# An attention and gated feed-forward stack in fp32 on one core: a norm's clamp and square moved to ScalarE, two tiled matmul stages made neighbours, and two copies reordered

## Chip, cores, metric

One Trainium2 chip, one of its cores. The time is the device time of one launch in microseconds (us), median over runs. Everything is computed in fp32.

## The reference

`x` is (4, 512, 128): four sequences (B) of 512 tokens. A small cross attention with a context comes first (the prologue here, under 3% of the time). Then a stack of six layers runs, each with a windowed attention of 16 heads of 64 and a gated feed-forward:

```python
def l2norm(t):
    return t / jnp.maximum(jnp.linalg.norm(t, axis=-1, keepdims=True), 1e-12)

def attn_layer(x, Wqkv, qs, ksc, Wo):
    q, k, v = jnp.split(x @ Wqkv, 3, -1)          # split in 16 heads of 64
    q = l2norm(q) * qs
    k = l2norm(k) * ksc
    q = q * cos * scale + rotate_half(q) * sin * scale
    k = k * cos * inv + rotate_half(k) * sin * inv
    out = local_attention(q, k, v)                # windows of 32, look back one window, softmax
    return out @ Wo

def ffn_layer(x, g, bln, W1, b1, W2, b2):
    a, gate = jnp.split((layernorm(x) * g + bln) @ W1 + b1, 2, -1)
    return a * gelu(gate) @ W2 + b2

for i in range(6):
    x = attn_layer(shift_tokens(x), ...) + x
    x = ffn_layer(shift_tokens(x), ...) + x
```

## The kernel before

The stack is cut into 192 units: 24 groups (a layer and a sequence), each of 8 units (4 tiles of 128 tokens times 2 halves of 8 heads). It is a software pipeline written out by hand: slot `n` of a long loop issues stages of several units. TensorE computes q and k of unit n, v of unit n, applies the attention weights of unit n-5 (`attend`), transposes o of n-6, makes the scores of n-3, transposes p of n-4, and then transposes k and q of n-2. `s = n % 8` is the slot within a group. Some slots have one more piece of TensorE work of the layer around the attention: s=0 `mean`, s=1 `variance`, s=2 and s=6 `project_out`, s=3 three `up` matmuls for the gate and one for a, s=4 and s=5 one `up` each, s=7 `down` (and every fourth group `fold_bias` in s=2). A 128x512 matmul in fp32 shows as two records in the profile.

`scores` and `attend` are the tiled stages: 16 matmuls each, whose weights are 32 columns wide and go to one of four column positions of the array (`tile_position=(0, WIN * w)`), shown as 128*32 in the profile. All other matmuls and transposes use the whole array, 128*128.

Other engines, in each slot:
- ScalarE (ACT): `copy_qT`, `norm_seed` (an inverse square root as Ln and Exp), `copy_v`, `copy_oT`, `squares` (the squares of q and k from PSUM), `copy_pT`, `copy_kB`, `fill_mask`, `exponentials`; in s=1 `square_d`, in s=2 `rstd_seed` (three operations), in s=3 three Gelus and two table loads.
- VectorE (DVE): `sum_p`, `newton` (a Newton step on the seed), `scale_k`, `scale_q`, `maxima`, `invert_sum`, `less_maxima`, `sum_squares`, `clamp_squares`, `scale_o` and the layer's sums and norms.
- GpSimd (POOL): the rotation of k and q, six operations a unit.
- SyncE (SP): the DMAs that spread v over the windows (`vs` to `vw`), 8 or 10 a unit, and the weights.

PSUM has two pairs of banks for q and k (`qk_bank0`, `qk_bank1`), one for scores (`sc_bank`) and a ring of three (`ring_bank`) that all other results share in the order of TensorE's program: the n-th use takes bank n % 3 and waits until the use three before it has been copied out (`ring_read`). So the order of TensorE's stages also says whose copy each of them waits for. `queries_keys(n)` waits until `scale_q(n-2)` has read its bank. Engines work through their programs in order, each at its own pace, held together by semaphores.

## Time and profile before

| | us |
|---|---|
| median of 3 runs (1822.89 to 1824.75) | 1823.85 |
| the profiled execution, its own time | 1824.23 |
| its span in the profile | 1822.2 |

| engine | busy us | share of the span |
|---|---|---|
| PE (TensorE matmul) | 1750.3 | 96% |
| DVE (VectorE) | 1619.0 | 89% |
| POOL (GpSimd) | 1500.4 | 82% |
| ACT (ScalarE) | 1327.5 | 73% |

The span divides in a prologue of some 50 us, the 192 slots that start a unit, and a tail in which the last units leave the pipeline. A matmul's end in the profile is modelled, so consecutive ones overlap; the distance from one start to the next is what it costs. PEld is the loading of weights, beside PE.

### The profile page before, as it was taken

Reading aid. Unit: us, or ns where it says so; the run is one execution under the profiler, and the core shown is the slowest. Engines: PE = TensorE matmul, PEld = TensorE weight load, DVE = VectorE, ACT = ScalarE, POOL = GpSimd, SP = SyncE. Lnnn points to the kernel's source line nnn. Section 1 sums busy time; section 2 is a strip of 40 time slices with the busy share of each in tenths; the row PEclk is TensorE's granted clock in tenths of the full one; section 3 lists DMA queues with packets and bytes.
Section 4 is the critical chain, followed back from the end, with each engine's and each line's share of the span. In section 5 each row is a group of like instructions: output and inputs, shape, how many; then the busy total and the mean of one; then the engine's idle time right before and its main releaser. Section 6 shows DMA issues by size and latency. Waiting matters only on the chain.

```text
span 1822.2 us, 48666 instructions
## 1 busy us (share of the span) xinstructions
PE 1750.3 (96%) x18122; PEld 1116.2 (61%) x18122; DVE 1619.0 (89%) x2782; ACT 1327.5 (73%) x2362; POOL 1500.4 (82%) x1204
## 2 busy tenths in 40 slices
PE   7699999999999999999999999999999999999986
PEld 6356666666666666666666666666666666666663
DVE  7799998999999989989999999899999998988874
ACT  3577877877778778778777777787776877877763
POOL 4799888888888888988888888888888888888860
PEclk9999999999999999999999999999999999999998
DMA  4132222222222222322223222222222222222221
GB/s 114 28 87 67 68 71 57 60 73 76 71 63 69 63 66 71 76 65 68 63 56 81 72 70 72 54 63 73 75 72 62 68 58 58 59 71 56 56 64 29
DMA packets 155273, 120.59 MB, mean 66 GB/s; under 512 B 42607, under 2 KB 151457, under 8 KB 154913
## 3 DMA queue, kind: packets, MB, share of 16 engines
q1 hardware_dynamic: 155041, 117.48, 25.1%
q8 instruction: 147, 2.41, 0.6%
q14 instruction: 85, 0.70, 0.1%
HBM read 18.79 MB, written 1.05 MB: 11 GB/s over the span
## 4 chain that ended last, share of the span: by engine, by line
PE 77%; DVE 13%; POOL 5%; issue 3%; SPq 1%; ACT 1%; DMA 1%; DVEq 0%; POOLq 0%; ACTq 0%
PE qk_bank L376 17%; PE ring_bank L448 10%; PE ring_bank L472 9%; PE ring_bank L389 8%; PE sc_bank L423 7%; PE ring_bank L516 6%; PE ring_bank L436 4%; PE ring_bank L399 3%; PE ring_bank L527 3%; PE ring_bank L461 3%; PE ring_bank L410 3%; DVE rn L842 2%; DVE step L837 2%; DVE o L898 2%; DVE qkn L858 2%
## 5 line engine op out<-in xcount | busy, mean ns | idle before, releaser
L1053 POOL TENSOR_TENSOR turned<-qkn,tables 128x512 f32<-128x512 f32 x384 | 489.3, 1274 | 209.8 <-DVE qkn L850 201.5
L1060 POOL TENSOR_TENSOR turned<-qkn,tables 128x512 f32<-128x512 f32 x384 | 496.7, 1294 | 0.0
L376 PE MATMUL qk_bank<-wqkv,xT 128*128 128x512 f32 x768 | 366.5, 600 | 18.8 <-DVE qkn L858 18.6
L1089 POOL TENSOR_TENSOR turned<-turned 128x512 f32<-128x512 f32 x192 | 255.0, 1328 | 15.1
L1096 POOL TENSOR_TENSOR turned<-turned 128x512 f32<-128x512 f32 x192 | 245.1, 1277 | 15.1
L448 PEld LDWEIGHTS ring_bank<-vw,pT 128*32 128x32 f32 x6144 | 156.6, 110 | 143.8 <-issue 143.7
L654 ACT ACTIVATE kB<-ring_bank 64x512 f32<-64x512 f32 x384 | 225.3, 587 | 23.5 <-PE ring_bank L410 21.2
L824 DVE TENSOR_REDUCE ss<-sq 128x16 f32<-128x1024 f32 x192 | 232.0, 1208 | 6.8 <-ACT sq L618 6.8
L627 ACT ACTIVATE vs<-ring_bank 128x512 f32<-128x512 f32 x192 | 114.7, 598 | 163.1 <-PE ring_bank L389 153.4
L898 DVE TENSOR_TENSOR o<-ring_bank,rr 128x512 f32<-128x512 f32 x192 | 132.1, 688 | 104.2 <-PE ring_bank L448 101.3
L389 PE MATMUL ring_bank<-wqkv,xT 128*128 128x512 f32 x384 | 216.1, 645 | 1.6 <-DVE x L978 1.6
L664 ACT ACTIVATE sc_bank<-mask_f 128x512 f32<-128x512 f32 x192 | 114.5, 596 | 136.0 <-DVE pr L873 135.6
L448 PE MATMUL ring_bank<-vw,pT 128*32 128x128 f32 x6144 | 208.4, 276 | 0.1
L423 PE MATMUL sc_bank<-kB,qT 128*32 128x128 f32 x6144 | 207.5, 276 | 0.3
L376 PEld LDWEIGHTS qk_bank<-wqkv,xT 128*128 128x128 f32 x768 | 131.2, 191 | 121.7 <-issue 93.4
L618 ACT ACTIVATE sq<-qk_bank 128x1024 f32<-128x1024 f32 x192 | 198.0, 1031 | 0.0
L423 PEld LDWEIGHTS sc_bank<-kB,qT 128*32 128x32 f32 x6144 | 156.0, 109 | 34.7 <-issue 34.7
L472 PE MATMUL ring_bank<-oT,wo 128*128 128x256 f32 x768 | 173.8, 379 | 0.0
L461 PEld LDWEIGHTS ring_bank<-ident,o 128*128 128x128 f32 x768 | 95.5, 141 | 102.1 <-issue 83.9
L472 PEld LDWEIGHTS ring_bank<-oT,wo 128*128 128x128 f32 x768 | 142.2, 190 | 18.1 <-DVE uT L956 0.8
L516 PE MATMUL ring_bank<-xnT,w 128*128 128x512 f32 x288 | 143.3, 609 | 8.5 <-DVE xnT L947 7.3
L850 DVE TENSOR_TENSOR qkn<-qk_bank,rn 128x512 f32<-128x512 f32 x192 | 132.9, 692 | 20.7 <-DVE rn L842 0.9
(169 smaller groups left out, 3129.3 us busy)
## 6 DMA issues: line engine op xcount, KB each, us to landing
vw<-vs SPq DMA_DIRECT2D x1152, 64.0 KB, 2.1
vw<-vs SPq DMA_DIRECT2D x672, 32.0 KB, 1.9
wqkv<-in_L_ffn_Wqkv_dram SPq DMA_DIRECT2D x20, 384.0 KB, 3.5
wo<-in_L_ffn_Wo_dram SPq DMA_DIRECT2D x20, 128.0 KB, 3.3
w<-in_L_ffn_W_dram SPq DMA_DIRECT2D x6, 341.0 KB, 3.4
wqkv<-in_L_ffn_Wqkv_dram SPq DMA_DIRECT2D x1, 1536.0 KB, 9.5
x<-in_x_dram SPq DMA_DIRECT2D x2, 512.0 KB, 4.7
out_dram<-x SPq DMA_DIRECT2D x4, 256.0 KB, 2.3
```

The costliest lines, as they stand in the source:

```text
L376: mm = pe.matmul(QK[u % 2][:, i * UW:(i + 1) * UW], tok, wqkv[:, layer % 2, cut:cut + UW], start=True, stop=True)
L389: pe.matmul(RING[i % RINGS][:, :], xT[:, b, t * P:(t + 1) * P], wqkv[:, layer % 2, cut:cut + UW], start=True, stop=True).then_inc(ring_mad ...
L423: mm = pe.matmul(heads(SC_BANK[WIN * w:WIN * (w + 1), k * P:(k + 1) * P]), qT[:, u % 2, k, WIN * w:WIN * (w + 1)], kB[:, HP * half + k, :, ...
L448: mm = pe.matmul(heads(RING[i % RINGS][WIN * w:WIN * (w + 1), k * P:(k + 1) * P]), pT[:, u % 2, k, WIN * w:WIN * (w + 1)], vw[:, u % 2, w, ...
L472: mm = pe.matmul(RING[i % RINGS][:, 0:HALF], wo[:, layer % 2, k, :], oT[:, k, HALF * h:HALF * (h + 1)], start=(k == 0), stop=(k == KO - 1))
L516: pe.matmul(RING[i % RINGS][:, :], w1[:, DFF * j + k * P:DFF * j + (k + 1) * P], xnT[:, :], start=True, stop=True).then_inc(ring_made[i % ...
L654: ev = act.activation(kB[64 * h:64 * h + 64, HP * half:HP * half + HP, h, WIN + P * t:WIN + P * t + P], RING[i % RINGS][64 * h:64 * h + 64 ...
L824: dve.tensor_reduce(ss[:, :], heads(sq[:, :]), AX.X, ALU.add).then_inc(ss_done, 1)
L1053: return pool.tensor_tensor(heads(turned[:, u % 2, 2 * i, :]), heads(qkn[:, u % 2, i * UW:(i + 1) * UW]), table.unsqueeze(1).to_broadcast( ...
L1060: return pool.tensor_tensor(halves(turned[:, u % 2, 2 * i + 1, :]), halves(qkn[:, u % 2, i * UW:(i + 1) * UW])[:, :, ::-1, :], table.rearr ...
L1089: pool.tensor_tensor(q, q, turned[:, u % 2, 1, :], ALU.add).then_inc(q_summed, 1)
L1096: pool.tensor_tensor(k, k, turned[:, u % 2, 3, :], ALU.add).then_inc(k_summed, 1)
```

## The change

Four edits:
- The norm's seed. `clamp_squares` (VectorE's maximum with the smallest norm) goes. ScalarE now reads the sums `ss` itself: Relu(ss - min), Ln with the minimum added back through its bias, Exp, and then the half square of the seed, `half_sq`. VectorE's Newton step has two operations in place of three. Each unit so has four small ScalarE operations in place of two, and two small VectorE operations in place of four. `ss` has two buffers.
- TensorE's order in a slot: v now comes ahead of `attend`, and `scores` right behind it, ahead of the transposes of o.
- ScalarE's order: the copy of p right behind that of o, and `squares` behind the copy of k.
- `vs` has seven slots in place of six, so `copy_v` waits for a DMA of one unit earlier. VectorE's `sum_p` of the next unit stands ahead of `scale_o`, except in s=3.

```diff
-VS = 6
+VS = 7
@@ tensor
                 queries_keys(n)
+                values(n)
                 attend(n - 5)
-                values(n)
+                scores(n - 3)
                 transpose_o(n - 6)
-                scores(n - 3)
                 transpose_p(n - 4)
@@ scalar
-                act.wait_ge(ssm_done, u + 1)
-                act.activation(lnn[:, u % 2, :], ssm[:, u % 2, :], ACT.Ln, scale=LN_SHIFT).then_inc(ln_done, 1)
-                act.wait_ge(ln_done, u + 1)
-                act.activation(seed[:, u % 2, :], lnn[:, u % 2, :], ACT.Exp, bias=shift_back[:, 0:1],
-                               scale=-0.5).then_inc(seed_done, 1)
+                act.wait_ge(ss_done, u + 1)
+                act.activation(above, ss[:, u % 2, :], ACT.Relu, bias=floor[:, 0:1]).then_inc(seed_part, 1)
+                act.wait_ge(seed_part, 4 * u + 1)
+                act.activation(above, above, ACT.Ln, bias=floor[:, 1:2], scale=LN_SHIFT).then_inc(seed_part, 1)
+                act.wait_ge(seed_part, 4 * u + 2)
+                act.activation(sd, above, ACT.Exp, bias=shift_back[:, 0:1], scale=-0.5).then_inc(seed_part, 1)
+                act.wait_ge(seed_part, 4 * u + 3)
+                act.activation(half_sq[:, u % 2, :], sd, ACT.Square, scale=0.5 ** 0.5).then_inc(seed_part, 1)
...
                 copy_oT(n - 6)
-                squares(n)
                 copy_pT(n - 4)
...
                 copy_kB(n - 2)
+                squares(n)
@@ vector
-                dve.scalar_tensor_tensor(out=step[:, :], in0=sd, scalar=-0.5, in1=sd,
-                                         op0=ALU.mult, op1=ALU.mult).then_inc(newton_done, 1)
-                dve.wait_ge(newton_done, 2 * u + 1)
-                dve.tensor_tensor(step[:, :], step[:, :], ssm[:, u % 2, :], ALU.mult).then_inc(newton_done, 1)
-                dve.wait_ge(newton_done, 2 * u + 2)
-                dve.scalar_tensor_tensor(out=r, in0=step[:, :], scalar=1.5, in1=sd,
-                                         op0=ALU.add, op1=ALU.mult).then_inc(rn_done, 1)
+                dve.wait_ge(seed_part, 4 * u + 4)
+                dve.scalar_tensor_tensor(out=step[:, :], in0=ss[:, u % 2, :], scalar=NORM_MIN ** 2, in1=half_sq[:, u % 2, :],
+                                         op0=ALU.max, op1=ALU.mult).then_inc(newton_done, 1)
+                dve.wait_ge(newton_done, u + 1)
+                dve.scalar_tensor_tensor(out=rn[:, u % 2, :], in0=step[:, :], scalar=1.5, in1=seed[:, u % 2, :],
+                                         op0=ALU.subtract, op1=ALU.mult).then_inc(rn_done, 1)
...
-                clamp_squares(n - 1)
...
+                if s != 3:
+                    sum_p(n - 4)
                 scale_o(n - 5)
```

TensorE's program, the start of a slot in the middle of the stack, before (qk_bank: q and k; `wqkv,xT` into a ring bank: v; `vw,pT`: attend; `ident,o`, `ident,pr`, `ident,turned`: transposes of o, p, and k; sc_bank: scores):

```order
L376 MATMUL qk_bank1<-wqkv,xT 128x512 x2
L448 MATMUL ring_bank0<-vw,pT 32x128 x16
L389 MATMUL ring_bank1<-wqkv,xT 128x512
L461 MATMUL ring_bank2<-ident,o 128x128 x4
L423 MATMUL sc_bank<-kB,qT 32x128 x16
L436 MATMUL ring_bank0<-ident,pr 128x128 x4
L410 MATMUL ring_bank1<-ident,turned 128x128 x4
```

The same place in the changed kernel:

```order
L374 MATMUL qk_bank1<-wqkv,xT 128x512 x2
L387 MATMUL ring_bank0<-wqkv,xT 128x512
L446 MATMUL ring_bank1<-vw,pT 32x128 x16
L421 MATMUL sc_bank<-kB,qT 32x128 x16
L459 MATMUL ring_bank2<-ident,o 128x128 x4
L434 MATMUL ring_bank0<-ident,pr 128x128 x4
L408 MATMUL ring_bank1<-ident,turned 128x128 x4
```

The two tiled stages now touch. In the ring, p's transposes took the bank of `attend` (read by VectorE's `scale_o`) and now take the bank of v (read by ScalarE's `copy_v`); k's transposes took v's bank and now take that of `attend`.

ScalarE's program from the copy of k in slot s=0 to that of v in s=1, before:

```order
L654 ACTIVATE kB<-ring_bank0 64x4x128 x2
L664 ACTIVATE sc_bank<-mask_f 128x512
L671 ACTIVATE pr<-pr 128x512
L645 ACTIVATE qT<-ring_bank1 128x512
L634 ACTIVATE lnn<-ssm 128x16
L636 ACTIVATE seed<-lnn,shift_back 128x16
L698 ACTIVATE dsq<-dT 128x512
L627 ACTIVATE vs<-ring_bank0 128x512
```

The same stretch in the changed kernel, without the copy of k at its head:

```order
L616 ACTIVATE sq<-qk_bank0 128x1024
L666 ACTIVATE sc_bank<-mask_f 128x512
L673 ACTIVATE pr<-pr 128x512
L647 ACTIVATE qT<-ring_bank1 128x512
L633 ACTIVATE lnn<-ss,floor 128x16
L635 ACTIVATE lnn<-lnn,floor 128x16
L637 ACTIVATE seed<-lnn,shift_back 128x16
L639 ACTIVATE half_sq<-seed 128x16
L700 ACTIVATE dsq<-dT 128x512
L625 ACTIVATE vs<-ring_bank2 128x512
```

The squares of q and k and two more small operations stand in this stretch now, between the copy of k and that of v.

VectorE's program from the sum of squares in s=1 to the scaling of k, before:

```order
L824 TENSOR_REDUCE ss<-sq 128x16
L830 TENSOR_TENSOR ssm<-ss,norm_min 128x16
L898 TENSOR_TENSOR o<-ring_bank2,rr 128x512
L880 TENSOR_REDUCE rs<-pr 128x8
L837 SCALAR_TENSOR_TENSOR step<-seed 128x16
L840 TENSOR_TENSOR step<-step,ssm 128x16
L842 SCALAR_TENSOR_TENSOR rn<-step,seed 128x16
L850 TENSOR_TENSOR qkn<-qk_bank0,rn 128x512
```

And changed:

```order
L827 TENSOR_REDUCE ss<-sq 128x16
L874 TENSOR_REDUCE rs<-pr 128x8
L892 TENSOR_TENSOR o<-ring_bank0,rr 128x512
L833 SCALAR_TENSOR_TENSOR step<-ss,half_sq 128x16
L836 SCALAR_TENSOR_TENSOR rn<-step,seed 128x16
L844 TENSOR_TENSOR qkn<-qk_bank0,rn 128x512
```

The sum over p (`rs`) comes ahead of the scaling of o, which waits for `attend`, and two small operations are gone.

## Rows read from the trace of the kernel before

**Rows 1.** Windows, 400 to 1600 us: busy time of PE, PEld, DVE, ACT, POOL; clock; DMA.
```profile
400.00:1600.00 1200.00, 1184.54 (x12409) 752.65 (x12408) 1100.57 (x1842) 911.85 (x1625) 1027.81 (x818) 1.00 0.26 67
```

**Rows 2.** The page: the span.
```profile
span 1822.2 us, 48666 instructions
```

**Rows 3.** Groups by line and shape, 400 to 1600 us: busy, mean ns, idle before.
```profile
L376 PE MATMUL qk_bank<-wqkv,xT 128*128 128x512 f32 x535 | 254.8, 599 | 12.5 <-DVE qkn L858 12.5
L830 DVE TENSOR_TENSOR ssm<-ss,norm_min 128x16 f32<-128x16 f32 x134 | 68.4, 510 | 4.6
```

**Rows 4.** Timeline of PE, one slot (s=4): start, us, engine, line, operation, tiles, count.
```profile
926.74 1.88 PE L376 MATMUL qk_bank<-wqkv,xT 128*128 128x512 f32 x4
928.55 1.08 PE L448 MATMUL ring_bank<-vw,pT 128*32 128x128 f32 x32
929.57 1.12 PE L389 MATMUL ring_bank<-wqkv,xT 128*128 128x512 f32 x2
930.53 0.60 PE L461 MATMUL ring_bank<-ident,o 128*128 128x128 f32 x4
931.06 1.08 PE L423 MATMUL sc_bank<-kB,qT 128*32 128x128 f32 x32
932.07 0.66 PE L436 MATMUL ring_bank<-ident,pr 128*128 128x128 f32 x4
932.56 0.60 PE L410 MATMUL ring_bank<-ident,turned 128*128 128x128 f32 x4
...
934.29 0.59 PE L376 MATMUL qk_bank<-wqkv,xT 128*128 128x512 f32 x1
```

**Rows 5.** Timeline of PE, s=3: matmuls and transposes without a tiled neighbour.
```profile
924.59 1.88 PE L516 MATMUL ring_bank<-xnT,w 128*128 128x512 f32 x4
926.30 0.60 PE L399 MATMUL ring_bank<-ident,turned 128*128 128x128 f32 x4
```

**Rows 6.** Timeline of PE, narrow windows: first and last four records of one attend.
```profile
936.11 0.32 PE L448 MATMUL ring_bank<-vw,pT 128*32 128x128 f32 x4
...
936.90 0.29 PE L448 MATMUL ring_bank<-vw,pT 128*32 128x128 f32 x4
937.12 0.70 PE L389 MATMUL ring_bank<-wqkv,xT 128*128 128x512 f32 x1
```

**Rows 7.** Timelines of DVE and of POOL, the same moment in s=5.
```profile
940.11 1.14 DVE L842 SCALAR_TENSOR_TENSOR rn<-step,seed 128x16 f32<-128x16 f32 x1
939.91 1.30 POOL L1089 TENSOR_TENSOR turned<-turned 128x512 f32<-128x512 f32 x1
```

**Rows 8.** Waits, 400 to 1600 us: in total, times, longest.
```profile
ACT vs L627 <- PE ring_bank L389: 102.7, 118, 2.7
DVE o L898 <- PE ring_bank L448: 66.1, 70, 2.2
```

**Rows 9.** Timeline of ACT, from s=0 into s=1.
```profile
969.54 1.19 ACT L654 ACTIVATE kB<-ring_bank 64x512 f32<-64x512 f32 x2 [0.64 <-PE ring_bank L410]
...
971.90 0.60 ACT L645 ACTIVATE qT<-ring_bank 128x512 f32<-128x512 f32 x1
972.59 0.22 ACT L634 ACTIVATE lnn<-ssm 128x16 f32<-128x16 f32 x1
972.84 0.31 ACT L636 ACTIVATE seed<-lnn,shift_back 128x16 f32<-128x16 f32 x1
973.05 0.61 ACT L698 ACTIVATE dsq<-dT 128x512 f32<-128x512 f32 x1
974.21 0.60 ACT L627 ACTIVATE vs<-ring_bank 128x512 f32<-128x512 f32 x1 [0.54 <-DMA vw<-vs]
```

**Rows 10.** Timeline of ACT, from s=3 into s=4.
```profile
921.30 1.03 ACT L618 ACTIVATE sq<-qk_bank 128x1024 f32<-128x1024 f32 x1
...
929.23 0.58 ACT L645 ACTIVATE qT<-ring_bank 128x512 f32<-128x512 f32 x1
930.79 0.60 ACT L627 ACTIVATE vs<-ring_bank 128x512 f32<-128x512 f32 x1 [0.53 <-PE ring_bank L389]
```

More of the change, by code:

```diff
@@ L107, in build @@
         turned = sb("turned", [P, 2, 4, UW])
-        ss = sb("ss", [P, 2 * HU])
-        ssm = sb("ssm", [P, 2, 2 * HU])
-        lnn = sb("lnn", [P, 2, 2 * HU])
+        ss = sb("ss", [P, 2, 2 * HU])
+        lnn = sb("lnn", [P, 2 * HU])
         seed = sb("seed", [P, 2, 2 * HU])
+        half_sq = sb("half_sq", [P, 2, 2 * HU])
         step = sb("step", [P, 2 * HU])
@@ L114, in build @@
         shift_back = sb("shift_back", [P, 1])
-        norm_min = sb("norm_min", [P, 2 * HU])
+        floor = sb("floor", [P, 2])
         qT = sb("qT", [P, 2, HP, P])
@@ L221, in build @@
         ss_done = sem("ss_done")
-        ssm_done = sem("ssm_done")
-        ln_done = sem("ln_done")
-        seed_done = sem("seed_done")
+        seed_part = sem("seed_part")
         newton_done = sem("newton_done")
@@ L624, in copy_v @@
                 if u >= VS - 2:
-                    act.wait_ge(vw_dma[u % 2], vw_count(u - VS + 2))
+                    act.wait_ge(vw_dma[(u - VS + 2) % 2], vw_count(u - VS + 2))
                 act.wait_ge(ring_made[i % RINGS], i // RINGS + 1)
@@ L632, in norm_seed @@
                     return
-                act.wait_ge(ssm_done, u + 1)
-                act.activation(lnn[:, u % 2, :], ssm[:, u % 2, :], ACT.Ln, scale=LN_SHIFT).then_inc(ln_done, 1)
-                act.wait_ge(ln_done, u + 1)
-                act.activation(seed[:, u % 2, :], lnn[:, u % 2, :], ACT.Exp, bias=shift_back[:, 0:1],
-                               scale=-0.5).then_inc(seed_done, 1)
+                above, sd = lnn[:, :], seed[:, u % 2, :]
+                act.wait_ge(ss_done, u + 1)
[6 more added lines that the diff above has]
+                act.activation(half_sq[:, u % 2, :], sd, ACT.Square, scale=0.5 ** 0.5).then_inc(seed_part, 1)
             def copy_qT(u):
@@ L756, in _ @@
             dve.memset(shift_back[:, :], 0.5 * float(np.log(LN_SHIFT))).then_inc(cst_ready, 1)
-            dve.memset(norm_min[:, :], NORM_MIN ** 2)
+            dve.memset(floor[:, 0:1], -NORM_MIN ** 2)
+            dve.memset(floor[:, 1:2], LN_SHIFT * NORM_MIN ** 2)
             dve.memset(mean_w[:, :], 1.0 / C).then_inc(cst_ready, 1)
@@ L823, in sum_squares @@
                 dve.wait_ge(sq_done, u + 1)
-                dve.tensor_reduce(ss[:, :], heads(sq[:, :]), AX.X, ALU.add).then_inc(ss_done, 1)
-            def clamp_squares(u):
-                if not 0 <= u < UNITS:
-                    return
-                dve.wait_ge(ss_done, u + 1)
-                dve.tensor_tensor(ssm[:, u % 2, :], ss[:, :], norm_min[:, :], ALU.max).then_inc(ssm_done, 1)
+                dve.tensor_reduce(ss[:, u % 2, :], heads(sq[:, :]), AX.X, ALU.add).then_inc(ss_done, 1)
             def newton(u):
@@ L982, in _ @@
                 g, s = n // UPG, n % UPG
-                sum_p(n - 5)
                 newton(n - 2)
@@ L990, in _ @@
                 if s == 1:
+                    finish(g - 3)
                     centre(g - 2)
@@ L1013, in _ @@
                     layer_norm(g - 2)
-                if s == 1:
-                    finish(g - 3)
+                    sum_p(n - 4)
         @block.gpsimd
```

2 lines of the change are left out of this document (removed).

## Prediction, on record before the run

> **What bounds the kernel now.** I read the windows first. Between 400 and 1600 us TensorE is busy 1184.5 of 1200 us at the full clock (1.00, so 2.4 GHz), VectorE 1100.6, GpSimd 1027.8, ScalarE 911.9 [rows 1]. The windows' sum says that TensorE is the bound and that only its own work, or its stalls, are worth time. The profiled execution took 1824.2 us, 2.0 more than its span [rows 2] and 0.4 more than the median; I work from 1824.2.
>
> Next the pace. q and k take four records a slot, and 535 of them lie in 1200 us [rows 3], so a slot takes 1200 / 133.75 = 8.97 us on average, 71.8 us a group of 8. Little of that is waiting: 1200 - 1184.5 = 15.5 us idle, of which 12.5 lie ahead of q and k and are put down to VectorE's scaling of q (L858) [rows 3]. A record runs some 0.16 us past the point where the next could start (0.60 us long, 0.44 apart in the transposes [rows 4, 5]), so some 28 such waits hide about 4.5 us more. Together 20 us in 16.7 groups, 1.2 a group; I use 1.3.
>
> Then TensorE's timeline of one slot, where the reader is to look at distances between starts, not at lengths. Four passes of 512 columns take 926.30 - 924.59 = 1.71 us where no tiled stage is near, and four transposes 926.74 - 926.30 = 0.44 [rows 4, 5]. Next to the tiled stages they take more:
> - q and k ahead of `attend`: 928.55 - 926.74 = 1.81, 0.10 more [rows 4].
> - v behind it: 930.53 - 929.57 = 0.96 for two passes, against 0.86: 0.10 more.
> - o's transposes ahead of `scores`: 931.06 - 930.53 = 0.53, 0.09 more. p's behind: 932.56 - 932.07 = 0.49, 0.05 more.
> - Inside `attend`, the first and last quadruples of records start 0.79 us apart, seven steps of 0.113; but from the last to v it is 937.12 - 936.90 = 0.22, 0.11 more [rows 6].
>
> So each trip into tiling and back costs about 0.10 in, 0.11 out and another 0.05 to 0.10 on the first full stage. A slot makes two trips.
>
> **The change, step by step.**
>
> *Tiled stages side by side.* One exit (0.11), the surcharge on v behind it (0.10) and one entry (0.09) go, and about 0.03 of the slower first quadruple: 0.33 us a slot, 192 x 0.33 = **63 us**. The exit behind `scores` and the entry behind v stay. From below: if only the visible surcharges on v and o vanish, 0.19 x 192 = 36 us. From above 0.11 + 0.10 + 0.10 + 0.10 = 0.41, 79 us. I take 0.33, since each term has its row. The Trainium skill, in "TensorEngine Tiling (Array Packing)", section "Key Properties", says that changing the tiling mode drains TensorE while moving among tiles of one mode does not. By that rule the two stages, both 128x32, need no drain between them, and the trace agrees with it in the surcharges.
>
> *VectorE.* The clamp of 0.51 us on average goes [rows 3], and one of three Newton steps. These are tiny operations that are long when they meet GpSimd: the last Newton step started at 940.11, ran 1.14 and ended at 941.25 beside a GpSimd operation that ended at 941.21 [rows 7]. So a chain of two costs 0.4 to 1.35 us, where one of three could meet GpSimd twice. Also `sum_p` (0.6 us) now fills the time that `scale_o` waited for `attend`, 66.1 us in 1200 [rows 8]. On the other side `attend` ends 0.87 us later in the slot (it starts at 1.72 + 0.96 = 2.68 instead of 1.81). In a short slot (s=0, 1, 4, 5; 934.29 - 926.74 = 7.55 us before, 7.22 after) the round from q and k over `attend`, o, Newton, and scaling k and q is then 3.9 + 0.6 + 1.3 + 1.4 = 7.2 us: as long as TensorE's slot. VectorE's stalls mostly vanish: **31 us** (24 x 1.3) come back, and I charge 0.15 a group again below.
>
> *ScalarE.* It gets two more small operations, and their dependence is a chain. Ln takes 0.22, Exp 0.31 [rows 9]; with starts 0.25 apart before, four of them with bias take 1.1 to 1.3, I take 1.2 against 0.55. The Trainium skill has a rule against this step: "ScalarE: Activation LUTs", section "Rules for kernel authors", gives relu and max to VectorE and budgets about 0.3 us for an ACTIVATE with a pointer as bias, which would make four of them about 1.2 us as well, an estimate by that page; the rows bear the price out, but VectorE's clamp was 0.51 here, not cheaper.
>
> ScalarE as a whole has room: 911.9 of 1200 busy, 102.7 of it idle ahead of the copy of v [rows 1, 8]. What counts is when the copy of v is done. Before, v's bank was next used by k's transposes; now p's transposes take it, which stand earlier. And the squares, 1.03 us [rows 10], now lie between the copies of k and v. I walk the places, with times from the slot's start; TensorE after the change: v 1.72, `attend` 2.68, `scores` 3.58, o's transposes 4.57, p's 5.06, k's 5.50.
>
> - s=1. In s=0 `mean` (0.86) stands ahead of k's transposes, so these start at 6.36, run 0.60 [rows 4], and ScalarE copies k from 7.0. From there to the copy of qT it was 971.90 - 969.54 = 2.36 us [rows 9]; now the squares add 0.93. Then qT 0.6, four small operations 1.2, `square_d` 0.6, copy of v 0.6: 7.0 + 2.36 + 0.93 + 3.0 = 13.3, less 7.22 is 6.1. p's transposes want the bank at 5.06: **1.0 us** of stall.
> - s=4. Before, qT's copy started 929.23 - 926.74 = 2.49 into the slot, right after the table load [rows 4, 10]. The squares now lie ahead of it, and it starts at 3.45 and ends at 4.05; `scores` want it at 3.58: 0.5. Then 3.95 + 1.2 + 0.6 = 5.8 for the copy of v against 5.06 + 0.5: 0.25. Together **0.75**. Before there was room: `scores` started at 4.32, v's copy at 930.79 still waited 0.53 for TensorE [rows 4, 10].
> - s=3. `rstd_seed` in s=2 stands behind the squares; v's copy ends about 5.2: **0.15**.
> - s=5, 0.15 from VectorE as above. s=2, 6, 7 are long (9 to 10 us) and cover everything.
>
> That is 2.05 a group, times 24: **49 us**. From below nothing, if ScalarE keeps ahead; from above, with 1.3 us for the four and 0.1 more on every copy, 3 us a group, 72 us.
>
> *Seven slots for v.* ScalarE waited 0.54 us for the DMA at 974.21 [rows 9]. In a shorter slot this wait would grow; with a unit more of distance it goes. Cover for anything left is TensorE's wait above. I cost it at nothing. If the DMA were late all the same, the copy of v and p's transposes are late next.
>
> Sum: 1824.2 - 63 - 31 + 49 = 1779.
>
> **Rivals.**
> - *ScalarE keeps up.* Its stalls at s=1 and s=4 don't come, as short slots give back what long ones hold. For it: 288 us idle in 1200. Against: the walk, slot by slot. 1824 - 63 - 31 = 1730, or 1761 if VectorE's stalls stay as they are. 0.2.
> - *ScalarE worse than walked*, stalls also in s=0 and s=5, as each short slot asks 6.5 to 6.8 us of it in 7.22: 3 us a group, 1802. 0.14.
> - *The drains don't go* (the surcharge belongs to new operands and not to the mode, so a smaller part goes): 0.1 a slot, 19 us, gives 1824 - 19 - 31 + 49 = 1823. For it: only one order of stages has ever been seen. Against: matmuls and transposes alternate elsewhere without any surcharge [rows 5]. 0.05.
> - *Slower: ScalarE becomes the bound of the short slots.* At the copy of v behind the chain of four. If each of the four took 0.5 us, its round of a short slot is 7.4 us and no slot is made up; at s=0, 1, 4 and 5 it costs about 1.1 each, 4.5 a group, 108 us: 1824 - 94 + 108 = 1838. It decides from (63 + 31) / 24 = 3.9 us of new stalls a group; Exp's 0.31 [rows 9] speaks against. 0.05. By the skill's rule that relu belongs on VectorE, this is the case that would follow.
>
> **How the numbers follow.** The forecast, 1765 to 1794, has 0.56. The range 1740 to 1805 takes in much of the first two rivals: about 0.8. A measurement of this kernel tells about 0.2% from no change. Faster by more than that: 0.56 + 0.2 + 0.14 and a little of the third, 0.92; within 0.2%: 0.03; slower: 0.05.
>
> **What would show it.** In TensorE's timeline: `attend` to `scores` about 0.90 us apart, `scores` to o's transposes 1.01, these then 0.49, v 0.96 ahead of `attend`; a slot without waits 0.33 shorter. In the waits: p's transposes on ScalarE's copy of v in s=1 and s=4, `scores` on qT in s=4. In the groups: four small operations of ScalarE at 0.2 to 0.3. Wrong would be: a first quadruple of `scores` as slow as before, no waits of TensorE on the copy of v, or waits on VectorE's scaling of q as often as before.

## The result, and the profile after

The changed kernel takes 1780.22 us (median of 4 runs, 1776.14 to 1781.41) against 1824.3 (now 4 runs, 1822.89 to 1830.04): ratio 0.9744, 95% interval 0.9726 to 0.9761. The forecast was 1779. The profiled execution took 1781.41 us.

The page of the changed kernel: span and busy time of each engine.

```profile
span 1779.4 us, 48666 instructions
...
PE 1709.0 (96%) x18122; PEld 1136.8 (64%) x18122; DVE 1370.6 (77%) x2399; ACT 1396.2 (78%) x2746; POOL 1499.9 (84%) x1204
```

VectorE falls from 89% to 77%, ScalarE rises from 73% to 78%: the two have passed each other. The window from 400 to 1600 us, to be read against [rows 1]:

```profile
400.00:1600.00 1200.00, 1187.20 (x12855) 788.41 (x12853) 949.06 (x1624) 987.60 (x1950) 1060.25 (x843) 1.00 0.26 69
```

TensorE is as busy as before, yet it issues more: 12855 records for 12409. What the change took out was busy time (drains inside matmuls) as well as idle time, so the busy share can't show the gain; the pace can. Groups of the same stretch, which answer to [rows 3]:

```profile
L374 PE MATMUL qk_bank<-wqkv,xT 128*128 128x512 f32 x552 | 259.9, 593 | 0.0
L833 DVE SCALAR_TENSOR_TENSOR step<-ss,half_sq 128x16 f32<-128x16 f32 x137 | 46.8, 342 | 6.5 <-ACT half_sq L639 5.3
L836 DVE SCALAR_TENSOR_TENSOR rn<-step,seed 128x16 f32<-128x16 f32 x137 | 26.1, 191 | 4.7
...
L639 ACT ACTIVATE half_sq<-seed 128x16 f32<-128x16 f32 x138 | 29.8, 216 | 4.4
```

There are 552 records of q and k for 535, and nothing idle ahead of them: TensorE no longer waits for VectorE's scaling of q. Newton costs VectorE 0.53 us a unit (0.34 and 0.19). Of ScalarE's four small operations the half square takes 0.22 us and the other three 0.30 to 0.31. The waits, 400 to 1560 us, show where TensorE waits instead:

```profile
PE sc_bank L421 <- ACT qT L647: 6.3, 17, 0.4
PE ring_bank L434 <- ACT vs L625: 5.9, 16, 0.4
```

Each comes once a group, at s=1 (vs) or s=4 (qT). TensorE's timeline of a slot without a wait (s=5), against [rows 4]:

```profile
916.34 1.88 PE L374 MATMUL qk_bank<-wqkv,xT 128*128 128x512 f32 x4
918.05 1.02 PE L387 MATMUL ring_bank<-wqkv,xT 128*128 128x512 f32 x2
919.01 1.08 PE L446 MATMUL ring_bank<-vw,pT 128*32 128x128 f32 x32
919.90 1.06 PE L421 MATMUL sc_bank<-kB,qT 128*32 128x128 f32 x32
920.89 0.66 PE L459 MATMUL ring_bank<-ident,o 128*128 128x128 f32 x4
921.38 0.60 PE L434 MATMUL ring_bank<-ident,pr 128*128 128x128 f32 x4
921.82 0.60 PE L408 MATMUL ring_bank<-ident,turned 128*128 128x128 f32 x4
```

Read the distances from start to start: q and k to v 1.71 (`attend` behind q and k took 1.81), v to `attend` 0.96, `attend` to `scores` 0.89 (1.02 to whatever followed it before), `scores` to o's transposes 0.99, these 0.49, p's 0.44 (0.49 before). And s=1, whose q and k start at 880.69, with its wait:

```profile
885.38 0.66 PE L459 MATMUL ring_bank<-ident,o 128*128 128x128 f32 x4
886.40 0.66 PE L434 MATMUL ring_bank<-ident,pr 128*128 128x128 f32 x4 [0.36 <-ACT vs L625]
```

p's transposes follow those of o by 1.02 instead of 0.49. The record of idle time says 0.36; the other 0.17 is the part by which o's record (0.66 long) runs past the point where the next stage could start. That is why I count stalls by starts. Two smaller ones stand beside it: in this slot `scores` start 1.01 behind `attend` instead of 0.89, as the copy of qT (ScalarE, below) ends only at 884.22, and k's transposes 0.49 behind p's instead of 0.44. The other end of this wait stands in ScalarE's timeline, from s=0 into s=1, against [rows 9]:

```profile
880.46 1.19 ACT L656 ACTIVATE kB<-ring_bank 64x512 f32<-64x512 f32 x2 [0.59 <-PE ring_bank L408]
881.67 1.02 ACT L616 ACTIVATE sq<-qk_bank 128x1024 f32<-128x1024 f32 x1
...
883.63 0.59 ACT L647 ACTIVATE qT<-ring_bank 128x512 f32<-128x512 f32 x1
884.11 0.30 ACT L633 ACTIVATE lnn<-ss,floor 128x16 f32<-128x16 f32 x1
...
885.25 0.61 ACT L700 ACTIVATE dsq<-dT 128x512 f32<-128x512 f32 x1
885.77 0.58 ACT L625 ACTIVATE vs<-ring_bank 128x512 f32<-128x512 f32 x1
```

From k's copy on nothing is idle, and the copy of v ends at 886.35, 0.05 us before p's transposes start.

For all that follows I took from each trace the start of q and k in every slot; the table gives mean slot lengths in the steady part of the stack, in us (one profiled execution of each kernel).

| kernel | s=0 | 1 | 2 | 3 | 4 | 5 | 6 | 7 | group |
|---|---|---|---|---|---|---|---|---|---|
| before | 7.56 | 8.04 | 10.55 | 10.41 | 7.55 | 8.21 | 10.25 | 9.27 | 71.84 |
| changed | 7.22 | 7.92 | 10.24 | 9.84 | 7.95 | 7.36 | 9.96 | 9.10 | 69.59 |
| no_join | 7.51 | 7.93 | 10.43 | 10.15 | 7.87 | 7.51 | 10.10 | 9.23 | 70.73 |
| order_back | 7.55 | 7.61 | 10.47 | 10.14 | 7.86 | 7.55 | 10.15 | 9.28 | 70.62 |
| order_only | 7.86 | 8.34 | 10.40 | 11.28 | 7.86 | 8.16 | 10.06 | 9.29 | 73.26 |
| seed_back | 7.45 | 8.69 | 10.34 | 11.36 | 8.10 | 7.88 | 10.07 | 9.30 | 73.20 |
| three_newton | 7.51 | 8.68 | 10.34 | 10.51 | 7.95 | 8.16 | 10.06 | 9.10 | 72.31 |
| squares_early | 7.87 | 7.86 | 10.30 | 10.27 | 7.87 | 7.86 | 9.95 | 9.10 | 71.08 |
| vs6 | 7.22 | 8.20 | 10.54 | 10.00 | 7.94 | 7.36 | 10.26 | 9.10 | 70.61 |
| o_first | 7.22 | 7.93 | 10.24 | 10.16 | 7.95 | 7.88 | 10.06 | 9.10 | 70.53 |
| late_dsq | 7.22 | 7.63 | 10.25 | 9.98 | 7.96 | 7.36 | 9.96 | 9.10 | 69.45 |
| dsq_dve | 7.22 | 7.57 | 10.24 | 10.45 | 7.95 | 7.36 | 9.96 | 9.11 | 69.86 |
| v_dve | 7.22 | 7.50 | 10.24 | 10.41 | 7.94 | 7.36 | 9.95 | 9.10 | 69.72 |
| v_dve_qT | 7.22 | 7.53 | 10.24 | 10.49 | 7.36 | 7.53 | 9.95 | 9.10 | 69.42 |

### The profile page after: what moved, and what is told of

It is laid out like the page before. It is cut to its first block, busy times and chain, and to the rows that moved or that the text cites. A ratio compares the mean times of both kernels' runs of the same rounds, so it can differ in the third digit from the quotient of the medians.

```text
span 1779.4 us, 48666 instructions
## 1 busy us (share of the span) xinstructions
PE 1709.0 (96%) x18122; PEld 1136.8 (64%) x18122; DVE 1370.6 (77%) x2399; ACT 1396.2 (78%) x2746; POOL 1499.9 (84%) x1204
## 4 chain that ended last, share of the span: by engine, by line
PE 75%; ACT 13%; POOL 5%; issue 4%; DVE 3%; ACTq 0%; DVEq 0%; POOLq 0%
PE qk_bank L374 13%; PE ring_bank L470 9%; PE sc_bank L421 8%; PE ring_bank L446 8%; PE ring_bank L387 7%; PE ring_bank L514 5%; PE ring_bank L459 5%; PE ring_bank L434 5%; PE ring_bank L408 4%; PE ring_bank L525 4%; PE ring_bank L397 3%; ACT sq L616 2%; ACT L718 2%; POOL turned L1047 2%; POOL turned L1054 2%
## 5 line engine op out<-in xcount | busy, mean ns | idle before, releaser
L692 ACT ACTIVATE oT<-ring_bank 128x512 f32<-128x512 f32 x192 | 114.5, 596 | 179.5 <-PE ring_bank L459 179.3
L387 PE MATMUL ring_bank<-wqkv,xT 128*128 128x512 f32 x384 | 197.6, 596 | 0.0
L421 PEld LDWEIGHTS sc_bank<-kB,qT 128*32 128x32 f32 x6144 | 169.4, 110 | 19.6 <-issue 19.5
L470 PE MATMUL ring_bank<-oT,wo 128*128 128x256 f32 x768 | 177.8, 385 | 0.0
L874 DVE TENSOR_REDUCE rs<-pr 128x8 f32<-128x512 f32 x192 | 130.6, 680 | 28.0 <-ACT pr L673 25.8
L397 PEld LDWEIGHTS ring_bank<-ident,turned 128*128 128x128 f32 x768 | 92.9, 141 | 87.7 <-issue 47.3
```

The lines of the kernel that those rows point to most:

```text
L387: pe.matmul(RING[i % RINGS][:, :], xT[:, b, t * P:(t + 1) * P], wqkv[:, layer % 2, cut:cut + UW], start=True, stop=True).then_inc(ring_mad ...
L421: mm = pe.matmul(heads(SC_BANK[WIN * w:WIN * (w + 1), k * P:(k + 1) * P]), qT[:, u % 2, k, WIN * w:WIN * (w + 1)], kB[:, HP * half + k, :, ...
L470: mm = pe.matmul(RING[i % RINGS][:, 0:HALF], wo[:, layer % 2, k, :], oT[:, k, HALF * h:HALF * (h + 1)], start=(k == 0), stop=(k == KO - 1))
```

## Experiments

Diffs are against the changed kernel, but for order_only. "Ratio" is that to the kernel before in the same round of measurements (its medians there: 1827.02, 1829.27 and 1828.51 us), with its 95% interval. The changed kernel was measured in the first round only, and the kernel before moved by up to 5 us from round to round, so differences in us to the changed kernel of some 5 us or less say nothing.

### One piece undone at a time

**no_join**: `scores` back behind the transposes of o, so that the two tiled stages are apart again.

```diff
                 attend(n - 5)
-                scores(n - 3)
                 transpose_o(n - 6)
+                scores(n - 3)
```

> The changed kernel with one thing undone: the transposes of o stand between attend and scores again, v stays ahead of attend, and the banks of the ring stay as they are. Theory (the price belongs to each trip into and out of the tiled mode): a second trip comes back, an exit of 0.11 and 0.05 on the transposes of o, and an entry of 0.09 with 0.02 on the first quadruple, 0.27 us a slot and 52 us over 192 slots. Since scores start 0.6 us later, the wait for the copy of qT in s=4 (0.55 us a group, 13 us) goes in return. So 1780 + 52 - 13 = 1819, between 1812 and 1832. Rival (the surcharge came from v and o meeting new operands, not from the mode): at most 19 us more, under 1800. In the timeline of TensorE the theory wants 0.53 us for the transposes of o and about 0.16 more than 0.90 from attend to the next stage.

Measured: 1802.65 us, ratio 0.987 (0.9844 to 0.9896). TensorE's timeline of its slot s=0:

```profile
888.86 1.08 PE L446 MATMUL ring_bank<-vw,pT 128*32 128x128 f32 x32
889.88 0.66 PE L459 MATMUL ring_bank<-ident,o 128*128 128x128 f32 x4
890.46 1.08 PE L421 MATMUL sc_bank<-kB,qT 128*32 128x128 f32 x32
891.47 0.66 PE L434 MATMUL ring_bank<-ident,pr 128*128 128x128 f32 x4
```

`attend` takes 1.02 again, o's transposes 0.58 and `scores` 1.01. A slot without waits is 7.51 for 7.22, 0.29 where 0.27 was expected, so the trip has the price that was read. But it is worth 22 us in the whole (27 by the slots, 1.14 a group), between the expectation and its rival: in s=1 the slot is 7.92 with the join and 7.93 without, because ScalarE's copy of v sets its end either way, and s=4 even favours no_join by 0.08. Where TensorE waits for another engine, shorter work on TensorE is a longer wait.

**squares_early**: the squares back between the copies of oT and pT.

```diff
                 copy_oT(n - 6)
+                squares(n)
                 copy_pT(n - 4)
...
                 copy_kB(n - 2)
-                squares(n)
```

> The changed kernel with ScalarE's squares between the copies of o and of p, as before. Theory (each copy out of the ring gates a stage of TensorE): the stretch from k's copy to v's is 0.93 us shorter, so the stalls in s=1 and s=4 (1.5 us a group) go; but p's copy then ends 7.4 us into the slot, and in s=0, 1, 4 and 5 the transposes of q, which take p's bank, want it at 6.8: 0.65 us each, 2.6 a group. Net 1.1 us a group slower, 27 us: 1807, between 1795 and 1815. Rival (only v's copy matters): 36 us faster, 1745.

Measured: 1811.68 us, ratio 0.9914 (0.9884 to 0.9944), as expected. Its one large wait:

```profile
PE ring_bank L397 <- ACT pT L682: 21.6, 68, 0.7
```

68 times in 1200 us, four a group: in each short slot the transposes of q want the bank of p's transposes, whose copy now comes a unit of squares later. All four short slots are 7.86 to 7.87, so the stalls in s=1 and s=4 have not come on top: the new wait has taken their place.

**vs6**: six slots for v.

```diff
-VS = 7
+VS = 6
```

> The changed kernel with six slots for v, so that v's copy again waits for a DMA one unit younger. I costed the seventh slot at nothing before. Theory: with six the DMA lands 9.1 us after attend of the slot before ends (in the trace of the kernel before: 974.21 against an attend that ended near 965.1); attend now ends at 3.8, so v's copy can't start before 12.9 - 7.2 = 5.6 us behind a short slot. Then p's transposes wait 1.2 us, in s=1 and s=5, less what is there already: 1.2 to 1.8 us a group, 1808 to 1825. Rival (the cost is hidden behind the waits that are there): 1780 within 4.

Measured: 1801.52 us, ratio 0.985 (0.9821 to 0.9878); 21 us for an edit that touches one number, somewhat less than expected. Waits, of ScalarE and then of TensorE behind it:

```profile
ACT vs L625 <- DMA vw<-vs: 35.5, 42, 1.9
```
```profile
PE ring_bank L434 <- ACT vs L625: 18.2, 32, 1.3
```

With six slots the copy of v waits for the DMA of the unit four before it, with seven for that of five before, which is issued earlier. p's transposes wait for the copy twice as often as in the changed kernel. s=1, 2, 3 and 6 are longer by 0.28, 0.30, 0.16 and 0.30; the expectation had named s=1 and s=5, and s=5 is unchanged.

**seed_back**: the clamp on VectorE, the three Newton operations and two small ScalarE operations, as before, with the new orders.

```diff
-                act.activation(above, ss[:, u % 2, :], ACT.Relu, bias=floor[:, 0:1]).then_inc(seed_part, 1)
...
-                act.activation(half_sq[:, u % 2, :], sd, ACT.Square, scale=0.5 ** 0.5).then_inc(seed_part, 1)
+                act.activation(lnn[:, u % 2, :], ssm[:, u % 2, :], ACT.Ln, scale=LN_SHIFT).then_inc(ln_done, 1)
...
+                dve.tensor_tensor(ssm[:, u % 2, :], ss[:, :], norm_min[:, :], ALU.max).then_inc(ssm_done, 1)
```

> The changed kernel with the norm's seed as before: the clamp on VectorE, two small operations on ScalarE, three Newton operations on VectorE. All orders and the seven slots of v stay. Theory A (both engines matter): ScalarE's chain is 0.65 us shorter, so the stalls in s=1 and s=4 shrink from 0.72 and 0.77 us to about 0.1 and 0.3; but VectorE's round in a short slot becomes 3.9 + 0.6 + 2.0 + 1.4 = 7.9 us against TensorE's 7.22, and waits on the scaling of q of up to 0.7 us come back in some of the four short slots. Net between -0.3 and +1.3 us a group: 1775 to 1810, centre 1793. Theory B (ScalarE alone sets the stalls, VectorE has room): 24 us less, 1756. Theory C (the seed's move is what made the kernel faster): back to 1815 or more.

Measured: 1867.85 us, ratio 1.023 (1.0199 to 1.0261). The largest miss of the study, in the range of theory C and not of theory A: the seed is worth 88 us here, and without it the change would be a loss. VectorE's timeline in a short slot whose q and k start at 889.03 us:

```profile
892.95 0.69 DVE L898 TENSOR_TENSOR o<-ring_bank,rr 128x512 f32<-128x512 f32 x1 [0.70 <-PE ring_bank L448]
893.55 0.54 DVE L837 SCALAR_TENSOR_TENSOR step<-seed 128x16 f32<-128x16 f32 x1
...
894.33 1.13 DVE L842 SCALAR_TENSOR_TENSOR rn<-step,seed 128x16 f32<-128x16 f32 x1
...
896.18 0.68 DVE L858 TENSOR_TENSOR qkn<-qk_bank,rn 128x512 f32<-128x512 f32 x1
```

GpSimd's timeline of the same moment:

```profile
892.77 1.29 POOL L1061 TENSOR_TENSOR turned<-qkn,tables 128x512 f32<-128x512 f32 x1
894.14 1.29 POOL L1090 TENSOR_TENSOR turned<-turned 128x512 f32<-128x512 f32 x1
```

The first Newton operation ends at 894.09, with the first GpSimd operation (894.06); the third at 895.46, with the second (895.43). VectorE's scaling of q ends at 896.86. TensorE could go on at 896.4, 0.44 behind q's transposes (895.95), but its timeline reads:

```profile
896.92 1.98 PE L376 MATMUL qk_bank<-wqkv,xT 128*128 128x512 f32 x4 [0.37 <-DVE qkn L858]
```

The round that begins with `attend` is longer than TensorE's slot. The Trainium skill, "SBUF — State Buffer", section "SBUF: two separate sides", describes VectorE and GpSimd as holding a shared pair of ports exclusively for a whole instruction, a VectorE operation with two SBUF inputs among those concerned. In both cases above VectorE's operation ends 0.03 us behind GpSimd's, which agrees with it.

**three_newton**: only the half square goes back, as a third operation of VectorE's chain; ScalarE keeps three small operations and VectorE has no clamp.

```diff
-                act.activation(half_sq[:, u % 2, :], sd, ACT.Square, scale=0.5 ** 0.5).then_inc(seed_part, 1)
...
+                dve.scalar_tensor_tensor(out=half_sq[:, u % 2, :], in0=seed[:, u % 2, :], scalar=0.5, in1=seed[:, u % 2, :],
+                                         op0=ALU.mult, op1=ALU.mult).then_inc(newton_done, 1)
```

> The changed kernel with the half square of the seed back on VectorE: three small operations on ScalarE, three Newton operations on VectorE, the clamp stays gone. It splits the 88 us that putting back the whole seed cost (1780 to 1868). Theory (each small VectorE operation may run up to 1.2 us beside GpSimd, and the round over attend, o, Newton, k and q is what TensorE's short slots wait for): Newton takes 1.9 instead of 0.8 us, the round 7.8 against 7.22, so about half of the 88 us: 1825, between 1805 and 1850. Rival (the clamp ahead of ScalarE's seed was the cost): 1780 to 1795. Rival (the third Newton operation is all of it): 1855 to 1870.

Measured: 1852.44 us, ratio 1.0143 (1.0118 to 1.0168). One operation on 128x16 numbers costs 72 us, most of the 88 of the whole seed; this is just above the expected range and below that of the rival. Its groups and waits, 400 to 1600 us:

```profile
L831 DVE SCALAR_TENSOR_TENSOR half_sq<-seed 128x16 f32<-128x16 f32 x133 | 113.9, 856 | 2.4 <-ACT seed L637 0.4
L837 DVE SCALAR_TENSOR_TENSOR rn<-step,seed 128x16 f32<-128x16 f32 x133 | 86.5, 650 | 4.6
```
```profile
PE qk_bank L374 <- DVE qkn L853: 22.3, 35, 0.7
```

The chain of three costs 0.86 + 0.28 + 0.65 = 1.78 us (means), that of two 0.34 + 0.19 = 0.53 in the changed kernel. Its length is not three times 0.17. It starts at o's scaling and runs into one GpSimd operation; in s=1, 2, 5 and 6 its third operation then meets a second one (1.13 us on average there, 0.17 to 0.18 in the other four slots), and s=1 and s=5 are the slots that grow most, by 0.76 and 0.80. The wait for q's scaling, gone in the changed kernel, is back, 22.3 us idle in 1200 for 12.5 before the change [rows 3].

**o_first**: `scale_o` ahead of `sum_p`, as before.

```diff
-                if s != 3:
-                    sum_p(n - 4)
                 scale_o(n - 5)
...
+                sum_p(n - 4)
```

> The changed kernel with VectorE's sum over p behind the scaling of o again. The sum takes 0.6 us; behind o it stands on the round of a short slot: 3.9 + 0.6 + 0.6 + 0.85 + 1.4 = 7.4 against TensorE's 7.22. s=1 and s=4 are longer already from ScalarE's waits, so the cost shows in s=0 and s=5: 0.2 to 0.6 us a group, 1785 to 1797. Rival (VectorE idles enough, 77% busy): 1780.

Measured: 1805.96 us, ratio 0.9882 (0.9858 to 0.9906): 25.7 us above the changed kernel, more than expected. By the slots it is 0.94 us a group, in s=5 (7.88 for 7.36), s=3 and s=6; s=0, where a part was expected, is unchanged. `sum_p` runs for nothing while VectorE waits for `attend`; behind `scale_o` its 0.6 us lie in the round that ends with q's scaling.

### The order alone, and the rest alone

**order_only**: the kernel before with only TensorE's new order (and one finishing step of VectorE put earlier in s=1, so that the new order of banks can run; the changed kernel has it there too, a fifth edit beside the four listed); **order_back**: the changed kernel with TensorE's old order.

```diff
@@ order_only, against before
                 queries_keys(n)
-                attend(n - 5)
                 values(n)
+                attend(n - 5)
+                scores(n - 3)
                 transpose_o(n - 6)
-                scores(n - 3)
```

> The kernel before with TensorE's new order alone (v, attend, scores, transposes of o); on VectorE only the last output's step moves ahead of centre, which matters in the last groups. Nothing else of the change. After the run with the old seed (1868 us) my theory is: side by side, attend ends at 3.85 us of the slot, and VectorE's round from there (o 0.6, three Newton operations up to 2.6, k and q 1.4, and here also the sum over p 0.6) is longer than TensorE's short slot of 7.22, so the tiled stages side by side lose time unless the seed moves: slower than before, 1850 to 1890, centre 1868. Rival (TensorE's own order is what gains, each part adds by itself): 63 us less than before less ScalarE's waits, 1765 to 1800.

> The changed kernel with TensorE's order as before (attend, v, transposes of o, scores); the seed, ScalarE's order and the seven slots stay. TensorE pays two trips again, but attend ends at 3.0 us of the slot and the transposes of o at 4.4. Theory: VectorE's round becomes 3.06 + 0.6 + 0.9 + 1.4 = 6.0 us and no longer waits are seen on it; p's transposes take attend's bank again, so the stall on v's copy goes, and 1.43 us of old stalls too. A group is then 70.2 us of TensorE's own work plus what little is left: 71.8 - 1.4 = 70.4, times 24: 1790, between 1785 and 1800. So the seed's move alone would have brought most of the gain. Rival (only the joined stages gain anything): 1820 or more.

Measured: order_only 1871.18 us, ratio 1.0232 (1.0213 to 1.0252); order_back 1800.74 us, ratio 0.9842 (0.982 to 0.9864). order_only lies where it was expected; order_back lies at the upper end of its range. With before and changed this makes a square:

| | old order | new order |
|---|---|---|
| old rest | 1.0 | 1.0232 |
| new rest | 0.9842 | 0.9744 |

The order alone is a loss of 2.3%, and a gain of 1% on top of the rest. The rest is the seed, ScalarE's order, the seventh slot of v and the earlier `sum_p` together; no kernel has the new seed alone with everything else as before. The waits of order_only, 400 to 1600 us, against [rows 8]:

```profile
DVE o L898 <- PE ring_bank L448: 124.3, 116, 1.9
PEld ring_bank L399 <- ACT pT L680: 63.0, 66, 1.1
...
PE ring_bank L516 <- DVE xnT L947: 17.8, 16, 1.4
```

VectorE waits 124.3 us for `attend` (66.1 before) as this ends 0.87 us later in the slot, and all that it does behind it comes later: the layer norm's xnT, for which `up` waits in s=3 (11.28 us, 10.41 before). q's transposes wait for the copy of p, as in squares_early, since here too the squares stand ahead of that copy. They take p's bank in the old order as well, where their weights waited 20.2 us in 1200 for it: the bank isn't new, but the time left for the copy is shorter.

### Could ScalarE's two waits be taken away as well?

The changed kernel's largest stalls are ScalarE's, in s=1 and s=4. Four kernels try to remove them.

**late_dsq**: `square_d` of s=1 behind the copy of v. **dsq_dve**: the same square made by VectorE instead.

```diff
@@ late_dsq
-                if s == 1:
-                    square_d(g - 2)
...
                 copy_v(n)
+                if s == 1:
+                    square_d(g - 2)
                 copy_oT(n - 6)
                 copy_pT(n - 4)
@@ dsq_dve, in VectorE's program
+                dve.tensor_tensor(dsq[:, :], dT[:, :], dT[:, :], ALU.mult).then_inc(dsq_done, 1)
```

> The changed kernel, with ScalarE's square of d (0.52 us, s=1 only) behind the copy of v instead of ahead of it. Theory (p's transposes wait for v's copy in s=1): v's copy ends 0.52 us earlier, p's transposes start at 5.2 instead of 5.71, 0.5 us a group, 12 us: 1768, between 1764 and 1772. Rival (the stall in s=1 stands on something else and moves on to the next wait, the copy of o or of k): 1780.

> The changed kernel, with the square of d on VectorE right behind centre (s=1), where VectorE stands idle for ScalarE's squares. ScalarE then has 0.52 us less ahead of v's copy. Theory: as with the square behind v's copy, 12 us less, but the VectorE operation has two inputs in SBUF and may meet GpSimd, 0.7 to 1.9 us, and then delays the sum of squares by up to 0.8 us: 1768 to 1785, centre 1772. Rival (VectorE's room is enough for any of it): the same as the other, 1768.

Measured: late_dsq 1776.35 us, ratio 0.9714 (0.9695 to 0.9733); dsq_dve 1785.52 us, ratio 0.9762 (0.9739 to 0.9785). Neither gained the 12 us that were expected. s=1 falls from 7.92 to 7.63 and 7.57, but s=3 rises from 9.84 to 9.98 and 10.45. late_dsq is the fastest measured, yet its interval overlaps that of the changed kernel, and its slots are only 0.14 us a group shorter, some 3 us. Its profiled execution also got through the prologue 3.6 us sooner (second unit at 53.3 us for 56.9), which the edit doesn't touch.

**v_dve**: VectorE copies v. **v_dve_qT**: that, and in s=4 the copy of qT ahead of the table load and the exponentials of s=3.

```diff
@@ v_dve: out of ScalarE's program, and ahead of sum_p and scale_o in VectorE's
-                copy_v(n)
...
+                copy_v(n)
                 if s != 3:
                     sum_p(n - 4)
                 scale_o(n - 5)
@@ v_dve_qT, further, in ScalarE's program
                 copy_qT(n - 3)
+                if s == 4:
+                    exp_table(g - 2)
+                    exponentials(n - 4)
...
-                if s == 3:
-                    exp_table(g - 2)
-                exponentials(n - 3)
+                if s != 3:
+                    exponentials(n - 3)
```

> The changed kernel with the copy of v out of the ring done by VectorE, ahead of its sum over p, in place of ScalarE. VectorE waits 0.9 us a slot for attend and is 77% busy. ScalarE has 0.49 us less a slot, and v's copy no longer stands behind its chain of the seed. Theory: p's stall in s=1 goes, 0.6 us, the one of scores in s=4 stays; VectorE's round may get 0.1 to 0.2 longer in s=1 and s=5. So 0.4 to 0.6 us a group: 1766 to 1771. Rival (VectorE's round is at its limit and the 0.6 us fall on it in full): 1790 or more.

> As the one before, and in s=4 ScalarE copies qT ahead of the table load and of the exponentials. scores of s=4 then find qT copied at 2.15 us of the slot instead of 3.98, so their stall of 0.55 us goes; VectorE's sum over p now ends about 4.6, and the scaling of q in s=4 0.3 later than TensorE would like. Theory: 0.2 to 0.4 us a group more than the one before, 1755 to 1764, faster than both kernels. Rival (the seed's wait takes the place of qT's): the same as the one before.

Measured: v_dve 1787.26 us, ratio 0.9782 (0.9758 to 0.9806); v_dve_qT 1778.11 us, ratio 0.9734 (0.971 to 0.9759). Both are slower than expected (1766 to 1771 and 1755 to 1764), and v_dve_qT can't be told from the changed kernel. s=1 falls to 7.50 and, in v_dve_qT, s=4 to 7.36: both waits for ScalarE are gone. But s=3 rises to 10.41 and 10.49, and in v_dve_qT s=5 by 0.17. In the waits of v_dve_qT one is left:

```profile
PE ring_bank L514 <- DVE xnT L952: 9.0, 13, 0.7
```

For v_dve, where the same wait takes 7.8 us, its source is read in VectorE's timelines of s=3 (first v_dve, whose q and k start at 900.00 us; then the changed kernel, 898.58):

```profile
900.65 1.80 DVE L941 TENSOR_TENSOR dsq<-dsq,xnT 128x512 f32<-128x512 f32 x1
...
904.17 0.69 DVE L890 COPY vs<-ring_bank 128x512 f32<-128x512 f32 x1
...
905.37 0.74 DVE L950 SCALAR_TENSOR_TENSOR xnT<-dT,cols,rstd 128x512 f32<-128x512 f32 x1
```
```profile
899.23 1.14 DVE L932 TENSOR_TENSOR dsq<-dsq,xnT 128x512 f32<-128x512 f32 x1
...
903.11 0.74 DVE L941 SCALAR_TENSOR_TENSOR xnT<-dT,cols,rstd 128x512 f32<-128x512 f32 x1
```

The norm's first operation takes 1.80 us in place of 1.14 and starts 0.65 into the slot like that of the changed kernel; xnT ends at 6.11 in the slot, not at 5.27, as v's copy lies ahead of it and the first operation is 0.66 longer (on average over the groups 1.38 for 1.16, and the end 5.89 for 5.29).

In v_dve_qT and dsq_dve it is another operation. There the norm's first two operations are over sooner, 3.18 and 3.11 into the slot for 3.48 in the changed kernel, and xnT starts at 4.53 on average in all three; but it takes 1.44 and 1.39 us instead of 0.76. One such slot of dsq_dve, VectorE and then GpSimd:

```profile
908.33 1.67 DVE L940 SCALAR_TENSOR_TENSOR xnT<-dT,cols,rstd 128x512 f32<-128x512 f32 x1
```
```profile
908.18 1.27 POOL L1082 TENSOR_TENSOR turned<-turned 128x512 f32<-128x512 f32 x1
```

xnT starts behind GpSimd's operation and ends 0.55 us after it. So a shorter s=1 by itself moves where VectorE's operations fall against GpSimd's. That this shift is all there is to the longer s=3 is argued from these rows; no kernel tests it by itself.

## Why the prediction was right

The forecast was 1779 for 1780.2, and the mechanism is the one that it gave; that the number came out to 1 us is luck in part, as said under the sum. Point by point, in us a group of 8 slots, by the table of slots; a stall is what a slot has above the same work in a slot without waits (7.55 before, 7.22 after, and the layer's extra matmuls by their own rows: 0.86, 3.46, 3.44, 0.86, 0.86, 3.46 and 2.58 in s=1 to s=7, of which the short slots hold 0.86 already; `fold_bias` 0.29 on average in s=2, 10.24 for 9.95 in a group without it).

- **Tiled stages side by side, 63 us (0.33 a slot).** Right. 7.55 to 7.22 is 0.33. no_join shows that 0.29 of it is the trip and 0.04 v's new place. But it is not a term that stands alone: taken out of the changed kernel it is worth 22 us, and added to the kernel before, with v's move, it costs 2.3%, 42 us.
- **VectorE's stalls, 31 us (1.3 a group).** Somewhat low: by the slots the kernel before had 1.65 (s=1 0.49, s=5 0.66, s=3 0.28, s=2 and s=6 0.11 and 0.10), about 40 us. Not all of it is VectorE's: 0.12 in s=1 lie ahead of q's transposes, whose weights wait for ScalarE's copy of p, so VectorE's part is some 1.5. The part ahead of q and k is gone, as their group shows. One reading was wrong: `sum_p` was to fill the 66.1 us that `scale_o` waited for `attend` [rows 8], but with `attend` later this wait grew, to 110.1 us in 1160. It costs nothing as long as what follows it fits into the slot. The reason was right and its weight wasn't seen: a third Newton operation costs 72 us in the new order, because there VectorE's round is longer than TensorE's slot. The text said that the round would be "as long as TensorE's slot" with two operations; that it left no room for a third one is what makes the seed a condition of the new order, not a gain beside it.
- **ScalarE's new waits, 49 us (2.05 a group).** The sum is right, by errors that cancel. s=4: 0.75 forecast, 0.73 found, `scores` on qT with 0.56 of it (912.52 - 908.40 = 4.12 against 919.90 - 916.34 = 3.56 in s=5); the 0.25 forecast for the copy of v there did not come as a wait, the rest is spread in parts of 0.02 to 0.07 over the stages behind. s=1: 1.0 forecast, 0.70 found (0.12 at `scores`, the rest at p's transposes), since the walk added copies by their length of 0.6 and they start 0.48 to 0.52 apart, and the four small operations took 1.14. s=3: 0.15 forecast, 0.02 to 0.05 found. s=5: 0.15 forecast, 0.14 found, but not from VectorE. s=2, 6 and 7, forecast as covered, have 0.13, 0.14 and 0.16. These four come from one stage of the new order, below. Together 2.04.
- **Seven slots for v, nothing.** Right: no wait for this DMA is left in the list of the changed kernel. It is no small matter either: with six slots the kernel takes 21 us more.
- **Sum.** 2.64 + 1.65 - 2.04 = 2.25 a group, and 71.84 - 69.59 = 2.25. Over 24 groups 54 us. The spans differ by 42.8: the second unit starts 5.6 us later than before (56.9 for 51.3), and the first two groups gain nothing. The prediction had 63 + 31 - 49 = 45 us, 1.87 a group, so it was 9 us low in the steady part, and took the gain for all 24 groups from the same start. These two errors cancel almost exactly, and the later start is a difference between executions that no edit explains.

The rivals fell as forecast. ScalarE doesn't keep up (its waits are there); it isn't the bound, with the four operations at 0.22 to 0.31; the drain goes. What the prediction had not seen is in s=2, 5, 6 and 7. TensorE's timeline of the end of s=7:

```profile
939.13 0.60 PE L408 MATMUL ring_bank<-ident,turned 128*128 128x128 f32 x4
939.65 2.81 PE L525 MATMUL ring_bank<-uT,w 128*128 128x512 f32 x6
```

k's transposes and `down` start 0.52 apart, and q's transposes follow at 942.30, 2.65 behind it. In no_join the same stage reads:

```profile
882.74 0.60 PE L408 MATMUL ring_bank<-ident,turned 128*128 128x128 f32 x4
883.17 2.74 PE L525 MATMUL ring_bank<-uT,w 128*128 128x512 f32 x6
```

0.43, and q's transposes at 885.75, 2.58 behind it. `down`, `project_out` and `up` take the bank of o's transposes; the join makes these 0.86 us later (4.55 into the slot for 3.69), and the copy of oT behind them ends just too late. In the same slot s=7 of the changed kernel:

```profile
938.96 0.60 ACT L692 ACTIVATE oT<-ring_bank 128x512 f32<-128x512 f32 x1 [1.87 <-PE ring_bank L459]
```
```profile
939.62 0.30 PEld L525 LDWEIGHTS ring_bank<-uT,w 128*128 128x128 f32 x2
```

The copy ends at 939.56 and the weights of `down` are loaded 0.06 later; in s=5 and s=6 the copy's end and the load of that slot's extra matmul are 0.05 to 0.06 apart as well. In no_join the copy of oT ends over 1 us ahead of these matmuls, their weights are loaded 0.11 ahead of them (0.00 to 0.03 in the changed kernel), and the 0.15 is gone. The profile lists no wait for it; the cause is read from these times and from the order of the ring.

## What to carry to other kernels

A stage's price on the busiest engine is only worth its price in slots where that engine doesn't wait; walk the other engines' rounds through the new order before counting it, and expect two edits to have no separate values (here +2.3% and -1.6% apart, -2.6% together). Where a chain of tiny dependent operations lies in such a round, its number counts more than their work, and moving one to an engine with slack can be worth more than the large edit (72 us for one operation here, 22 for the join). In all four kernels that removed a wait of s=1, part of it or more was given back in s=3, so compare slot by slot and not in the total alone.
